# The ring tile between the MLP's two norms moves into the attention that follows

## What is computed

```
# layer 0, per image
xp = x @ w_in + b_in
h = gelu(batchnorm(depthwise_conv3x3(x)))
offset, mask = h @ w_off + b_off, softmax over 9 taps (h @ w_msk + b_msk)
y = (sum over 9 taps of mask * bilinear sample of xp at the offset) @ w_out + b_out
x = x + gamma1 * layer_norm(y)
x = x + gamma2 * layer_norm(gelu(x @ w_fc1 + b_fc1) @ w_fc2 + b_fc2)
# layer 1, per image, t = tokens of x
t = t + causal_attention(layer_norm(t))
t = t + top2_experts(layer_norm(t))
```

## Time and profile before

| | |
|---|---|
| median of 3 runs | 8872.07 us |
| the profiled execution | 8881.66 us |
| its span | 8879.9 us |
| busy: POOL | 6554.4 us, 74% |
| busy: DVE | 5563.6 us, 63% |
| busy: PE | 5273.8 us, 59% |
| busy: ACT | 2767.3 us, 31% |
| granted TensorE clock | 0.781 of full speed |

### The profile page before, as it was taken

One profiled execution on the slowest core, in us unless ns is written; L12 is line 12 of the kernel. 1 busy time (PEld: TensorE's weight loads), 2 busy tenths in 40 slices (PEclk: granted clock), 3 DMA queues, 4 the chain that ended last, 5 costly groups with the idle time before them and its releaser, 6 DMA issues.

```text
span 8879.9 us, 85702 instructions
## 1 busy us (share of the span) xinstructions
PE 5273.8 (59%) x24752; PEld 3409.6 (38%) x24752; DVE 5563.6 (63%) x12091; ACT 2767.3 (31%) x6449; POOL 6554.4 (74%) x6898
## 2 busy tenths in 40 slices
PE   4456575555755576555665567654757556564567
PEld 2234353333533354333443344432434333342345
DVE  4666666666666666666576656765666666665554
ACT  2223232323323233322333233332323233332233
POOL 6777777777777777777777777777777777777771
PEclk7778787777877788777887788876878778776778
DMA  7333333232333323333333333333233333222220
GB/s 104 72 75 69 74 70 78 66 75 69 70 77 68 76 66 73 75 72 71 68 77 70 74 68 73 75 75 68 67 79 70 73 68 65 73 65 65 62 64 15
DMA packets 851881, 625.60 MB, mean 70 GB/s; under 512 B 551018, under 2 KB 734562, under 8 KB 851472
## 3 DMA queue, kind: packets, MB, share of 16 engines
q0 software_dynamic: 221200, 452.62, 21.0%
q1 hardware_dynamic: 629600, 167.72, 11.4%
q10 hardware_dynamic: 672, 0.24, 0.0%
HBM read 549.46 MB, written 70.57 MB: 70 GB/s over the span
## 4 chain that ended last, share of the span: by engine, by line
POOL 59%; issue 22%; PE 9%; DVE 5%; DMA 4%; SPq 1%; ACT 1%; POOLq 0%; DVEq 0%; another core or an unknown queue 0%; ACTq 0%
POOL ring L707 59%; DMA ring<-column_table,idx_r 3%; PE bank L1508 2%; PE bank L1544 2%; DVE y L1042 1%; PE bank L1517 1%; PE bank L1432 1%; PE bank L1684 1%; PE bank L1596 1%; PE bank L1661 1%; SPq L523 0%; DMA wts_r<-corner_weight 0%; SPq L493 0%; DVE ring L1032 0%; DMA tokens<-z 0%
## 5 line engine op out<-in xcount | busy, mean ns | idle before, releaser
L707 POOL DMA_INDIRECT ring<-column_table,idx_r x6860 | 6530.9, 952 | 2146.0 <-issue 2069.6
L1032 DVE TENSOR_TENSOR ring<-ring,bank 128x4608 f32<-128x4608 f32 x196 | 970.1, 4949 | 1017.7 <-POOLq L718 1016.6
L1042 DVE TENSOR_REDUCE y<-ring 128x128 f32<-128x4608 f32 x196 | 1571.1, 8016 | 16.8 <-remote 14.6
L1489 PE MATMUL bank<-ident,xn 112*128 112x112 f32 x224 | 54.9, 400 | 1722.5 <-DVE xn L968 1722.5
L1508 PE MATMUL bank<-kT,qT 128*112 128x448 f32 (+3 forms) x1792 | 824.7, 552 | 159.2 <-DVE arena L1144 152.2
L1544 PEld LDWEIGHTS bank<-v,pT 112*112 112x112 f32 x6496 | 817.7, 181 | 264.2 <-issue 186.1
L1544 PE MATMUL bank<-v,pT 112*112 112x128 f32 x6496 | 851.7, 278 | 57.1 <-DVE pT L1177 57.0
L1144 DVE TENSOR_SCALAR_CACHE_REDUCE arena<-bank 112x448 f32<-112x448 f32 x672 | 416.2, 623 | 524.6 <-PE bank L1508 495.4
L1517 PE MATMUL bank<-ident,arena 112*112 112x112 f32 x3248 | 495.6, 273 | 395.4 <-ACT arena L828 395.3
L1489 PEld LDWEIGHTS bank<-ident,xn 112*128 112x128 f32 x224 | 37.1, 217 | 1731.7 <-issue 1731.7
L1432 PE MATMUL bank<-xflat,stripes 116*128 116x448 f32 (+1 forms) x1120 | 586.9, 649 | 110.7 <-ACT xflat L790 110.6
(11 more groups left out here) (179 smaller groups left out, 7291.8 us busy)
## 6 DMA issues: line engine op xcount, KB each, us to landing
ring<-column_table,idx_r POOLq DMA_INDIRECT x6860
xflat<-dense_rows SPq DMA_DIRECT2D x56, 406.0 KB
column_table<-proj SPq DMA_DIRECT2D x196, 112.0 KB
corner_weight<-wts_s SPq DMA_DIRECT2D x56, 252.0 KB
wts_r<-corner_weight SPq DMA_DIRECT2D x196, 72.0 KB
hT<-dense_rows SPq DMA_DIRECT2D x224, 56.0 KB
tin<-tokens SPq DMA_DIRECT2D x56, 224.0 KB, 3.1
out<-xn SPq DMA_DIRECT2D x56, 224.0 KB
```

The lines of the kernel that those rows point to most:

```text
L707: pool.indirect_dma_start(ring[:, r, e * CORNERS:(e + 1) * CORNERS, :].rearrange("p s c -> p (s c)"), None, source, bass.IndirectOffsetOnA ...
L1032: dve.tensor_tensor(corners, corners, wts_p.unsqueeze(2).broadcast_to([128, GP * CORNERS, CG]), ALU.mult)\
L1042: dve.tensor_reduce(y[:, k % BLK % 2].rearrange("p (g c) -> p g c", g=G), ring[:, bass.ds(t % RING, 1)].rearrange("p o (g e) c -> p (o g) ...
```

## The change

Tile 0 of the half is no longer done by the MLP before. Each half now has its own tiles in its own attention and experts: half 0 tiles 0, 1, 2 as `first`, `second` and a new `extra`, and tile 3 as `third`; half 1 tiles 4 and 5 as `first` and `second`, and tile 6 as `third`. `extra` is multiplied behind q = 2 and summed behind q = 3. In the last slot half 0 has tiles 0 and 1, then 2; half 1 is as before. SP asks for indices, ACT for weights and PE for projections in the same new order. At the start the dense pass of chunk 0 comes ahead of tile 0 and that of chunk 1 ahead of tile 1.

```diff
                             None if fixed and 2 * NJ * p + f >= CHUNKS else (p, f)
                             for f in (2 * n + 1 + h, 2 * n + 2 + h))
                         g = i * NJ + j
-                        first, second, third, between = (
-                            ((p, n, 1), (p, n, 2), (p, n, 3), (p, n, 4)),
-                            ((p, n, 5), None, (p, n, 6), (p, n, BLK)))[h]
+                        first, second, extra, third = (
+                            ((p, n, 0), (p, n, 1), (p, n, 2), (p, n, 3)),
+                            ((p, n, 4), (p, n, 5), None, (p, n, 6)))[h]
                         if last:
 
-                            first, second, third, between = (
-                                (None, (p, n, 1), (p, n, 2), None),
-                                (None, (p, n, 4), (p, n, 5), None))[h]
+                            first, second, extra, third = (
+                                ((p, n, 0), (p, n, 1), None, (p, n, 2)),
+                                (None, (p, n, 4), None, (p, n, 5)))[h]
                         if att:
-                            attention(i, j, h, s, (p, fronts[h]), first, second, now)
+                            attention(i, j, h, s, (p, fronts[h]), first, second, extra, now)
                         else:
                             tile(*first)
+                            dense(now)
                             tile(*second)
-                            dense(now)
+                            tile(*extra)
                         experts_front((i, j) if att else None, (p, fronts[h]) if live[h] else None, third,
                                       2 * s + h, g if att else 0, now)
                         if last:
                             tile(p, n, k1 - 1)
-                        mlp(s, n, h, last, (p, fronts[h] + 1), g + 1 if att else 0, between, then)
+                        mlp(s, n, h, last, (p, fronts[h] + 1), g + 1 if att else 0, then)
 
             first_image()
             for f in range(1, LEAD):
                 experts_front(None, (0, f), None, 0, 0, None)
-            tile(0, 0, 0)
             dense((0, 0))
             slots(0)
             for p in range(1, PAIRS):
                 slots(p)
             i, j = attended(PAIRS, -1)
-            attention(i, j, 0, SLOTS, (PAIRS, 0), None, None, None)
+            attention(i, j, 0, SLOTS, (PAIRS, 0), None, None, None, None)
             experts_front((i, j), None, None, 2 * SLOTS, i * NJ + j, None)
...
-            def attention(i, j, h, s, fronts, first, second, now):
+            def attention(i, j, h, s, fronts, first, second, extra, now):
                 if first:
                     tile(*first)
                 if second:
                     tile(*second)
-
-            def mlp(s, n, half, last, fronts, n_att, between, then):
+                if extra:
+                    tile(*extra)
+
+            def mlp(s, n, half, last, fronts, n_att, then):
                 k0, k1 = PARTS[half]
                 if then:
...
-                if between:
-                    p, _, k = between
-                    keep_weights(p, n, k + 1)
...
                     if q == 1 and second:
                         tile(*second)
+                    if q == 3 and extra:
+                        tile(*extra)
...
                 step.did(shifted(1))
-                if between:
-                    tile(*between)
                 dve.wait_ge(fc2_made, FIRST + s * 2 + half + 1)
                 dve.tensor_tensor(z[:, k0:k1, :],
...
                     if second and q == 1:
                         sum_up(*second)
+                    if extra and q == 2:
+                        multiply(*extra)
+                    if extra and q == 3:
+                        sum_up(*extra)
...
                     if q == 1 and second:
                         tile(*second)
+                    if q == 3 and extra:
+                        tile(*extra)
```

2 lines of the change are left out of this document (1 added, 1 removed).

## The result

The changed kernel takes 8895.28 us, the median of 11 runs (8884.32 to 8901.46); the kernel before, on the same chip, 8872.73 us, the median of 11 (8859.56 to 8880.12). The ratio is 1.0025 with a 95% interval of 1.0016 to 1.0034, that is +22.5 us, between 14 and 30. I had forecast +5 us, within a range that ends at +26. The time lies inside the range, but past the 18 us that I had called "same": it is slower by 0.25%.

A forecast was written before the change was run, and what follows sets the result against it. POOL's back-to-back gathers bound the kernel: 51.8 us ahead, 8649 of gathers, 178.7 behind. To 8872 us came +8 (start), -3 (end), 0 (middle) and 0 (meetings), giving 8877 us, range 8860 to 8898.

The forecast's parts named there:

- same: Whole kernel: a change within 18 us (0.2%) can't be told from none; chance 0.84, forecast and nothing moves together.
- What bounds the kernel: Whole run: POOL's gathers go back to back, 8649 us, with 51.8 us ahead of them and 178.7 behind.
- Part 1, the MLP: Between the MLP's norms: the removed tile's 13.1 us lay under a wait for PE; about 1 us shorter a half.
- Part 2, the attention: One more tile in each attention lengthens it by 10 us in half 0 and 4.1 us in half 1.
- Part 3, the ring: Ring tiles in the middle: every place is free before POOL needs it again, so no stall, 0 us.
- Part 4, the start: Tile 5's index load at the start comes late and delays POOL by 8 us, bounds 4 and 13.
- Part 5, the end: Chain ahead of tile 192's multiply: 3 us won, at most 4.85; the program behind it is the same.
- Part 6, the meetings: Row loads meeting POOL's landing wait ahead of each tile's seventh gather: 0 us, bounds -12 and +20.
- The rivals: Whole kernel: nothing moves 8872 us (0.14), slower by transfers meeting 8910 (0.10) or dry ring 8980 (0.02), faster end 8856 (0.04).

The follow-up runs named there:

- New start only: The kernel before with only the change's start order (a dense pass ahead of tile 0, another ahead of tile 1): 8881.45 us, 1.0019 of before.
- rows early: The changed kernel with chunk 0's rows loaded ahead of the last front's table fills and stores instead of behind them: 8868.14 us, 1.0005 of before.
- old start: The changed kernel with before's start order (tile 0 ahead of the first dense pass, tiles 1 and 2 ahead of the second): 8865.86 us, 1.0003 of before.
- one pass ahead: The changed kernel with the second dense pass behind the first attention's three tiles, only the first ahead of tile 0: 8878.04 us, 1.0018 of before.

## Why the prediction was 17.5 us too low

**What bounds the kernel** was right, on the chips where before takes some 8870 us. Waits put on POOL at the start and stalls taken from it behind the start both showed in the time of the whole kernel.

**Part 1, the MLP.** Right. The second z sum waits for PE in all 56 MLPs, 11.9 us each:

```profile
DVE z L1090 <- PE bank L1478: 667.9, 56, 13.8
```

**Part 2, the attention.** Half 1's price was about right: its four seven-chunk attentions took 80.2 to 81.9 us with the second tile, before 76.5 to 78.9, which is 1.4 to 5.0 us each where I took 4. In half 0 I had charged 2 us for the extra multiply. In the attention of the earlier trace rows it cost 0.7 (the last t1 ends at 4584.93 us, before at 4584.54), in two others of seven chunks 3.5 and 3.7:

```profile
4584.58 0.35 DVE L1187 SCALAR_TENSOR_TENSOR t<-bank,rinv,tin 112x128 f32<-112x128 f32 x1 [2.20 <-PE bank L1545]
```

**Part 3, the ring.** Right. Behind tile 5 POOL waits for no free place. The smallest distance from a sum to the next gather into its place is 34.4 us for tile 2, still at the start, and 52.4 from there on.

**Part 4, the start**, is the step that failed. Its mechanism was right and its cost too small: I took 8 us, bounds 4 and 13; 18.5 were measured at tile 5's first gather. The chain that I gave was the right one and its terms can be compared:

| term | forecast, us | measured, us |
|---|---|---|
| rows used by DVE | 198.5 (204 at latest) | 206.24 |
| first dense pass, use to multiply | 24.0 | 25.6 |
| tile 0 summed | 235.6 | 244.8 |
| from there to the end of the second pass | 35.5 | 38.3 |
| tile 1 summed | 284.2 | 296.1 |
| tile 5's first gather | 287.3 | 299.40 |

7.7 of the 12 missing us are one sentence: "so 188.7 + 9.8 = 198.5". I took the 9.8 us from issue to use of a load that stood behind tile 0's index load, and gave it to one that stands right behind the stores. I had written that those stores were in flight, and allowed 5.5 us for them; it was 7.7. In the earlier trace rows a better measure was there: the rows were used at 207.54, 19.7 us behind the issue of drow's store at 187.82. With that distance the forecast would have been 207.5. "New start only" shows that an earlier issue behind the stores gains nothing, "rows early" that an issue 19.2 us earlier, ahead of the last front's stores, gains 17.6.

The other 4.4 us are the passes: the first was 1.6 us longer, the second 4.6 (254.49 to 283.12, 28.6 us), of which 1.9 came back since its rows were there sooner behind tile 0's sum (9.7 us against 11.5). I had one duration for a dense pass, 24.0 us. These new rows are before's first pass, after's first and after's second:

```profile
207.00:232.00 25.00, 12.82 (x21) 4.39 (x21) 2.17 (x4) 11.77 (x15) 18.92 (x20) 0.70 0.19 53
...
206.00:232.00 26.00, 14.06 (x20) 4.70 (x20) 1.82 (x4) 11.95 (x16) 19.73 (x21) 0.63 0.20 54
...
254.00:283.00 29.00, 17.04 (x20) 5.69 (x20) 1.60 (x3) 11.77 (x15) 21.92 (x24) 0.50 0.19 52
```

PE's granted clock was 0.70, 0.63 and 0.50 of full speed. Its steps of four multiplies take 3.35 us at half speed and 1.77 at full speed, with the same gap ahead of them, here from after's two passes (granted clock 1.00 in the first of these steps, 0.50 in the second):

```profile
214.99 1.77 PE L1433 MATMUL bank<-xflat,stripes 116*128 116x448 f32 x4 [1.83 <-ACT xflat L787]
...
263.25 3.35 PE L1433 MATMUL bank<-xflat,stripes 116*128 116x448 f32 x4 [1.83 <-ACT xflat L787]
```

The Trainium skill (TensorE: Matmul & The Clock Gate, section "What's actually happening") says that the array runs at 1.2 or at 2.4 GHz by how busy it has lately been; the two durations, 1.9 to 1, agree. A pass cost 24.0 us in before, where the clock rose for three of its five steps, and 28.6 where it stayed at half (all of 29 us at 0.50 in after's second). Both lengths came with either order of the start: in "old start", which keeps before's order here, the first pass took 28.6 us too, and in "new start only" the two took 28.6 and 24.2. So I put this down to the execution rather than to the change; with one trace of each kernel that is argued, not shown.

And one sentence was wrong in kind: "Tile 4 is 1.5 us late, which lies inside that." POOL waited 12.5 us ahead of tile 4 and another 7.7 ahead of tile 5. The two add up to the lateness of the second, as I had it, but the first is the larger part of it and stands alone in "one pass ahead", which costs 8 to 24 us.

**Part 5, the end.** Up to tile 192 it was right: that tile is multiplied 1.7 us behind its last gather, before 4.85:

```profile
8586.21 4.95 DVE L1031 TENSOR_TENSOR ring<-ring,bank 128x4608 f32<-128x4608 f32 x1 [13.55 <-POOLq L718]
```

That is 3.1 us of the 3 forecast, and in the two kernels without landing stalls it is 6.9 us with before's order against 1.7 with the changed one. Behind tile 192 I had put nothing, since the program is the same; there the trace of after is 9 us shorter, as told with the result. That term was left out, and its cause stays open.

**Part 6, the meetings.** Right in the trace, 27.5 us beyond 0.3 against 28.2. With the landing wait moved the changed order gains 27.8 us (old start) and before's 15.9, a difference of 12 us with intervals of some 8 on either part, so whether the changed order has more stalls stays open. So does the part of the 22.5 us beyond 18.5 - 3.1 = 15.4, which is 7 us and, if the shorter tail is counted as won, 16: the interval goes from 14 to 30.

**The rivals.** None of them came. I had weighed a slower outcome at 0.12 and tied it to meetings of transfers in the middle. What came is slower, and most of it came from my own forecast's start: with its upper bound of 13 us and the 3 won at the end it reached only +10, and the time stayed inside my range by the allowance of 20 us for meetings, which did not come. That part is luck. The bound of 13 was too tight since the landing behind the stores was bounded by a guess and not by a row, and the dense pass had no bound at all.

## What to carry to other kernels

Moving a load up in a queue moves its data only as far as what stands ahead of it in that queue allows: here the rows were used 18 to 21 us behind the issue of the last store ahead of them, however soon they were issued. Read when the stores ahead of it land, not how long the load took in its old place. Where the bound engine runs without slack, look for the places where it has never yet waited but is one place in the order away from it, above all at the start, and where a later wait swallows what is won earlier. And before adding work under other work's cover, look at the bound engine's own small stalls: here a wait set four gathers later was worth 16 to 28 us in four pairs of kernels, about as much as the change cost.

## What was not expected of the hardware

- One chip runs the kernel before in 14365 us and two others in 8873 and 8862. The slow one's granted clock is 0.663 against 0.773 in the old start's executions, and its chain of waits is another. The cause stays open.
- The same PE instructions behind tile 192 took 195.9 and 186.4 us in the profiled executions of before and after, at clocks of 0.77 and 0.80. The ten traces split by the order of tiles ahead of them, all but one. The cause stays open.
- The four hT loads took 6.0 to 7.0 us to issue right behind the last front's stores (four traces), and 2.5 to 3.6 us where some 9 us lay between (four).
